# First batch of a two-layer transformer kernel: order of its first transfers, of the split of the values' weights, and of the weight ring's refill

## The reference, cut to what matters

```python
L0_attn: q, k, v = x @ wq.T, x @ wk.T, x @ wv.T        # 16 heads, 4 key/value heads, 128 wide
         q, k = rope(q), rope(k)
         o = chunked linear attention with decay per head; return o @ wo.T
L0_ffn:  W = (w_int - 128) * scale                     # gate, up: 2048 x 512, down: 512 x 2048
         return (silu(x @ Wg.T) * (x @ Wu.T)) @ Wd.T
L1_attn: 32 heads of 16, 8 key/value heads, causal softmax, rope on pairs
L1_ffn:  thought = layernorm(x)[:, -1] @ agg_w + agg_b; four steps of a small MLP on it
         out = layernorm(x + sigmoid(x @ gate_w + gate_b) * (thought @ bc_w + bc_b))
```

## Time and profile before

| | |
|---|---|
| median of three runs | 4269.03 us (4269.03, 4260.94, 4269.23) |
| profiled execution | 4257.74 us, span 4256.0 us |
| mean granted TensorE clock | 0.949 |
| data moved | 579.13 MB, mean 136 GB/s |

### The profile page before, as it was taken

The page is one execution under the profiler, slowest core; times in us unless marked ns, Lnnn a source line. Parts: engine busy times, 40 slices in busy tenths (PEclk is TensorE's granted clock), DMA queues, the critical chain, the costliest instruction groups (busy, mean ns, idle before and its releaser), DMA issues.

```text
span 4256.0 us, 53470 instructions
## 1 busy us (share of the span) xinstructions
PE 3761.6 (88%) x19048; PEld 2722.4 (64%) x19048; DVE 2366.8 (56%) x4206; ACT 1626.2 (38%) x2748; POOL 1352.6 (32%) x1637
## 2 busy tenths in 40 slices
PE   6877899999999999999999999999999999978640
PEld 4756676577766776577766776677757776654310
DVE  5644565455654665456654665456644665365369
ACT  4422334524353434434353434434353435423112
POOL 2421442235312441244212541145213531121125
PEclk9989999999999999999999999999999999987765
DMA  6456433254324433253324432343325441332313
GB/s 235 163 202 233 159 138 135 75 195 156 130 85 149 173 115 134 86 204 137 131 85 167 163 133 100 130 176 136 130 74 183 141 155 66 109 121 70 109 40 119
DMA packets 173764, 579.13 MB, mean 136 GB/s; under 512 B 14680, under 2 KB 14936, under 8 KB 168127
## 3 DMA queue, kind: packets, MB, share of 16 engines
q1 hardware_dynamic: 169806, 568.37, 37.4%
q10 hardware_dynamic: 3696, 7.34, 0.5%
HBM read 490.19 MB, written 84.93 MB: 135 GB/s over the span
## 4 chain that ended last, share of the span: by engine, by line
PE 67%; DVE 16%; ACT 6%; issue 5%; POOL 4%; DMA 2%; SPq 0%; DVEq 0%; ACTq 0%; POOLq 0%
PE ps_P L1720 25%; PE ps_Y L1720 11%; PE ps_E L1720 5%; PE ps_O L1720 4%; PE ps_O L1911 4%; PE ps_E L1893 3%; PE ps_T L1872 3%; POOL pT_lo L801 3%; PE ps_T L1720 3%; DVE pf L1278 2%; PE ps_T L1876 2%; ACT probs L1046 1%; DVE stats L1185 1%; ACT pT_hi L931 1%; DVE row_max L1386 1%
## 5 line engine op out<-in xcount | busy, mean ns | idle before, releaser
L1720 PE MATMUL ps_P<-XnT_hi,w_ring 128*128 128x512 f32 x3328 | 1080.2, 406 | 64.9 <-DVE XnT_lo L1161 14.5
L1720 PEld LDWEIGHTS ps_P<-XnT_hi,w_ring 128*128 128x128 f32 x3328 | 608.7, 191 | 230.1 <-issue 72.2
L1720 PE MATMUL ps_P<-XnT_lo,w_ring 128*128 128x512 f32 x1664 | 659.2, 396 | 0.0
L1386 DVE TENSOR_REDUCE row_max<-ps_T 128x1 fp32r<-128x384 f32 (+3 forms) x768 | 425.5, 595 | 275.9 <-PE ps_T L1876 275.8
L1046 ACT ACTIVATE probs<-ps_E 128x512 f32<-128x512 f32 (+2 forms) x768 | 362.5, 524 | 449.3 <-PE ps_E L1893 301.3
L801 POOL TENSOR_TENSOR pT_lo<-pf,pT_hi 128x512 fp32r<-128x512 f32 x320 | 411.2, 1293 | 300.3 <-ACT pT_hi L931 295.8
L819 POOL TENSOR_SCALAR_AFFINE_SELECT probs<-probs 128x512 f32<-128x512 f32 x256 | 163.2, 638 | 1031.8 <-ACT probs L1046 1031.8
L873 POOL TENSOR_TENSOR hT_lo<-hf,hT_hi 128x512 fp32r<-128x512 f32 x128 | 164.7, 1287 | 639.3 <-ACT hT_hi L931 639.3
L1720 PEld LDWEIGHTS ps_P<-XnT_lo,w_ring 128*128 128x128 f32 x1664 | 317.6, 191 | 70.8
L1720 PE MATMUL ps_Y<-w_big,hT_hi 128*128 128x512 f32 x896 | 333.3, 418 | 25.7 <-DVE y_acc L1410 12.6
L792 POOL TENSOR_TENSOR sines<-swapped,sinT 128x512 f32<-128x512 f32 x160 | 214.4, 1340 | 377.3 <-ACT swapped L931 369.0
(11 more groups left out here) (286 smaller groups left out, 7027.7 us busy)
## 6 DMA issues: line engine op xcount, KB each, us to landing
w_ring<-split_dram SPq DMA_DIRECT2D x412, 512.0 KB, 3.4
w_big<-split_dram SPq DMA_DIRECT2D x64, 2048.0 KB, 7.7
dec<-decay SPq DMA_DIRECT2D x32, 1024.0 KB, 4.9
split_dram<-w_ring SPq DMA_DIRECT2D x58, 512.0 KB, 4.1
split_dram<-w_big SPq DMA_DIRECT2D x36, 512.0 KB, 4.4
wo1w<-split_dram SPq DMA_DIRECT2D x8, 2048.0 KB, 7.7
gatew<-split_dram SPq DMA_DIRECT2D x7, 2048.0 KB, 9.8
X<-x SPq DMA_DIRECT2D x8, 1024.0 KB, 9.8
```

The lines of the kernel that those rows point to most:

```text
L1386: dve.reduce_max(row_max[:, g % 2, i_, m0:m0 + len(heads)], ps[TB[half]][:, 0:len(heads) * w].rearrange("p (n s) -> p n s", s=w), AX_X)\
L1720: last = pe.matmul(dst, stat[s_], mov[m_], start=first_ and k == 0, stop=last_ and k == n - 1)
```

## The change

- The first batch's tokens come as four transfers of 256 KB, each with a semaphore of its own; `ident` goes out behind the first of them on its own semaphore, and TensorE and ScalarE wait for that alone at the start.
- The rope tables are issued behind two raw pieces and ahead of the other two; the decay table behind "pro". The seven other constants are issued behind the last group's blocks, and waited for ahead of "ho" (ScalarE, VectorE) and in iteration 1 (TensorE).
- "pro" splits u0 to u7 only. V's four pieces are split behind units 0 to 3 of group 0, each after that unit's ring piece.
- In slots 36 to 43 of the first iteration SyncE waits until the slot's writes have landed and issues `next_unit` for that slot; the wait for all slots and the loop behind the 48 slots go.

```diff
 def first_pieces():
-    out = {("pro",): [("u", j) for j in range(RING)] + [("w", BIG_V, k) for k in range(4)]}
+    out = {("pro",): [("u", j) for j in range(RING)]}
...
-                out["p", g, u] = [("u", NU * g + u + RING)]
+                out["p", g, u] = [("u", NU * g + u + RING)] + ([("w", BIG_V, u)] if g == 0 and u < 4 else [])
...
-            tokens_in(0)
-            for dst, src in ((ident[:, :], identity), (mask[:, :], causal), (ident_b[:, :], identity_b),
-                             (rope1[:, :, :, :].rearrange("p a t d -> p (a t d)"), rope1_tables),
-                             (gate_bias[:, :], gate_b.partition_broadcast(P)), (dsc[:, :], down_scale.partition_broadcast(P)),
-                             (gsc[:, :], gate_scale), (usc[:, :], up_scale)):
-                sp.dma_start(dst, src).then_inc(const_in, 16)
-            for r in range(RAW):
+            for t in range(NT):
+                sp.dma_start(X[0][:, t, :], x[0, t * P:(t + 1) * P, :]).then_inc(*x0_in[t].hit(0))
+                if t == 0:
+                    sp.dma_start(ident[:, :], identity).then_inc(ident_in, 16)
+            for r in range(2):
                 piece_in(r)
             tables(0)
-            decay_in(0, 0)
+            for r in range(2, RAW):
+                piece_in(r)
             for n in range(NB + 1):
                 c = n - 1
                 if n == 0:
                     first(("pro",))
+                    decay_in(0, 0)
...
                     if n == 0:
+                        for dst, src in ((mask[:, :], causal), (ident_b[:, :], identity_b),
...
+                            sp.dma_start(dst, src).then_inc(const_in, 16)
                         first(("ho",))
...
                         if n == 0:
                             first(("slot", s))
+                            if q == NQ - 1 and i < 8:
+
+                                k = UNITS_A + UNITS_C + 8 * q + i
+                                slot = slot_of[0, k]
+                                sp.wait_ge(*unit_out[slot].need(unit_out[slot].dims[0] - 1))
+                                next_unit(n, k)
                             if s == SLOTS - 1:
-
-                                for slot in range(RING):
-                                    sp.wait_ge(*unit_out[slot].need(unit_out[slot].dims[0] - 1))
...
-                if n == 0:
-                    for k in range(UNITS_A + UNITS_C + 24, UNITS):
-                        next_unit(n, k)
...
-            act.wait_ge(const_in, N_CONST)
+            act.wait_ge(ident_in, 16)
...
                 if n == 0:
+                    act.wait_ge(const_in, N_CONST)
                     first(("ho",))
...
-            dve.wait_ge(const_in, N_CONST)
             for n in range(NB + 1):
                 c, d = n - 1, n - 2
                 if n == 0:
-                    dve.wait_ge(*x_in[0].need(0))
                     for t in range(NT):
+                        dve.wait_ge(*x0_in[t].need(0))
                         measure("xa", 0, t, X[0][:, t, :])
...
                 if n == 0:
+                    dve.wait_ge(const_in, N_CONST)
                     first(("ho",))
...
-            pe.wait_ge(const_in, N_CONST)
-            pe.wait_ge(act_const_in, 1)
+            pe.wait_ge(ident_in, 16)
...
+                if n == 1:
+                    pe.wait_ge(const_in, N_CONST)
+                    pe.wait_ge(act_const_in, 1)
```

More of the change, by code:

```diff
@@ L370, in raw, with tokens_at @@
             return (raw_a if r % RAW < 2 else raw_b)[:, r % 2, :]
-        const_in, act_const_in = sem("s_const_in"), sem("s_identr")
+        const_in, act_const_in, ident_in = sem("s_const_in"), sem("s_identr"), sem("s_ident_in")
+        x0_in = [count(f"x0_in{t}", 1, step=16) for t in range(NT)]
         pool_const = sem("s_pool_const")
         x_in = [count(f"x_in{n}", NB // 2, step=16) for n in range(2)]
+        def tokens_at(n):
+            return n // 2 - (n % 2 == 0)
         x2_out, x2_in = count("x2_out", NB, step=16), count("x2_in", NB, step=16)
@@ L515, in build @@
         block = ctx.enter_context(nc.Block())
-        N_CONST = 16 * 8
+        N_CONST = 16 * 7
         @block.sync
@@ L566, in tokens_in @@
             def tokens_in(n):
-                sp.dma_start(X[n % 2][:, :, :], x[n, :, :].rearrange("(t p) d -> p t d", p=P)).then_inc(*x_in[n % 2].hit(n // 2))
+                sp.dma_start(X[n % 2][:, :, :], x[n, :, :].rearrange("(t p) d -> p t d", p=P)).then_inc(*x_in[n % 2].hit(tokens_at(n)))
             def decay_in(n, g):
@@ L676, in _ @@
                     if n == 0:
+                        for dst, src in ((mask[:, :], causal), (ident_b[:, :], identity_b),
+                                         (rope1[:, :, :, :].rearrange("p a t d -> p (a t d)"), rope1_tables),
+                                         (gate_bias[:, :], gate_b.partition_broadcast(P)), (dsc[:, :], down_scale.partition_broadcast(P)),
+                                         (gsc[:, :], gate_scale), (usc[:, :], up_scale)):
+                            sp.dma_start(dst, src).then_inc(const_in, 16)
                         first(("ho",))
@@ L1430, in behind @@
                         if t == 0:
-                            dve.wait_ge(*x_in[(n + 1) % 2].need((n + 1) // 2))
+                            dve.wait_ge(*x_in[(n + 1) % 2].need(tokens_at(n + 1)))
                         measure("xa", n + 1, t, X[(n + 1) % 2][:, t, :])
```

## The result

The changed kernel takes 4255.03 us (median of 13 runs, 4247.53 to 4268.45), the kernel before in the same comparison 4267.78 (13 runs). The ratio is 0.9972, 95% interval 0.9962 to 0.9981: 12 us or 0.28% faster. The prediction was 4250, in a range that holds the measured time. 12 us gained stand against 16.0 forecast. One of the 13 runs before took 5294.37 us, a slow run, and the ratio is of fast runs alone.

The account below looks back on a forecast made before the run. The prediction took the kernel as bound by TensorE's matmuls, untouched by the change; 5.6 us at the start plus 10.4 from the ring made 16.0, from 4266 to 4250 us. The range was 4238 to 4262.

Parts of the forecast that it names:

- Ring: Passage to the second batch: slot-by-slot refill removes 7.85 us of waiting and keeps TensorE's clock up, 10.4 us gained.
- rival 3: Second batch's first projections: the waiting goes but the lower clock stays; 13.5 us gained in all, 4252.5; chance 0.12.
- Start: First batch up to its first blocks: values products end at 57.4 us instead of 63.04, 5.6 us gained.
- Front: First batch's token statistics: the fourth aggregate starts at 6.9 us instead of 11.69, 4.7 us gained.
- Constants late: Seven constants issued behind the last group's blocks land before their first reader, at no cost, with 18 us margin.
- Decay table among the pieces: First batch, behind "pro": the 1 MB table among the weight pieces delays V's last piece by 2.7 us.
- Pace of the pieces: First batch's weight loads and splits: a piece every 1.93 us, set by DMA; at 2.6 us the start gives nothing.
- rival 1: First batch's start: pieces slow to 2.6 us each, so the start gives nothing; 10.4 us in all, 4255.6; chance 0.24.
- Rival 4: First batch's start: ring unit, rope and raw buffer wait in a circle; kernel 9.6 us slower, 4275.6; chance 0.04.
- Values cold: First batch's four values products, after TensorE stands still: the first takes 4.60 us, all four 12.8 us.
- Rival 2: First batch's start: TensorE keeps its clock before the values, pieces take 1.7 us; 19.8 us gained, 4246; chance 0.12.
- Past the first blocks: From 63 to 404 us: engine order unchanged, so the start's lead passes through; later batches keep their length.

Follow-up runs that it names:

- e2: The changed kernel with the ring refill put back as before; 2.6 us (0.06%) under the kernel before, with an interval that includes no change.
- after again: The changed kernel, unchanged, run again for a second profile and more runs; median 4257.21 us.
- e1: The kernel before with the slot-by-slot ring refill alone; 9.8 us faster by the ratio, 11.4 by the medians.
- e5: The changed kernel with the first tokens as one 1 MB transfer, ident behind it; the fourth aggregate starts at 9.32 us.
- e3: The kernel before with tokens by tile and late constants only; ratio 0.9991 with an interval that reaches 1.0000.
- e10: The changed kernel with the decay table issued behind V's last piece; 4255.54 us in one timed run.
- e6: The changed kernel with the decay table issued ahead of "pro", as before the change; 4249.74 us.
- e9: Against the changed kernel: V split behind units 0 and 1, u5 to u9 behind units 2 to 4, later pieces behind later groups' units, decay first; 4248.15 us.
- e7: Against the changed kernel: "pro" splits five ring pieces, then V's four; u10 to u12 in group 0's blocks, decay first; first blocks at 55.15 us.
- e8: Against the changed kernel: "pro" splits five ring pieces, V's four behind units 0 and 1, u10 to u12 in group 0's blocks, decay first; first blocks at 52.58 us.
- e4: The changed kernel with V's four pieces back in "pro", decay table still behind "pro"; 3 to 5 us under the changed kernel by the medians.
- e6b: The same kernel as e6, timed again beside the changed kernel; 4254.81 us, against 4257.21 for the changed kernel.

## Why the prediction was right, and where it was wrong

**Ring, 10.4 us forecast: right.** D went from 30.16 to 19.86, 10.3 us, in every kernel with the new refill (19.69 to 19.86) and in none without it. The waiting went and the clock stayed up: rival 3, the lower clock that stays, is out. Nothing else became late; V's 2 MB, issued at 442.92, is not in the chain: the values products there wait for VectorE, as before.

**Start, 5.6 us forecast: wrong.** e2 gives 2.6 us, not clear of no change; by the marks it is 1.2 us (C is 63.5 in the mean of after, after again and e2, 64.7 in the mean of before and e1). Its terms:

- *Front, 4.7 forecast, 3.3 measured* (B 15.74 in the mean of the same three, 19.04 in that of before and e1). I took the four tiles to land as fast as one transfer of 1 MB. In the first profile their statistics start 1.1 to 2.1 us apart (3.65, 5.79, 6.89, 8.20), the fourth at 8.20, a little behind the bound of 7.9 that I had given. The DMA views of 0 to 6 us are in the last part. The Trainium skill, page "DMA: Bandwidth & Descriptors", section "Bandwidth", has 138 GB/s at 64 KB and 341 at 1 MB, from transfers issued by GpSimd, and no row between; the estimate from it, 1.3 us less for the front, is nearly what came (1.4). That the number fits may be chance, since SyncE issues the transfers here and other loads stand behind them. I had set it aside with a row in which 256 KB pieces moved at 389 GB/s, but there many transfers, 512 KB ones among them, were in flight. Where I would not follow the rule is in batching to 1 MiB: e5 did this and was later.
- *Constants late, 0: right.* With them late e3 has a C-B of 45.56, with them early the kernel before and e1 have 45.37 and 45.99, and the changed kernel's first piece of "ho" starts at 254.72, without a wait for the seven constants, the last of which is issued by 234.63.
- *Decay table among the pieces, 2.7 forecast, 5.2 measured* (C-B 47.8 against 42.5 with the table ahead). This is the largest error. I charged its bytes. It is in the one queue ahead of loads on which ScalarE and VectorE wait, and its place costs twice its bytes. e10 confirms that: the same bytes behind V3's piece cost the first blocks nothing.
- *Pace of the pieces, 1.93 us each: right where the table is out of the way.* e6's two pieces per unit take 3.79 us. With the table in the queue the eight pieces from u7 (27.11) to V3 (47.98) take 2.6 us each, the very pace at which rival 1 has the start give nothing, and 2.4 in the two other traces. The measured 4255.03 also lies nearest to rival 1's 4255.6. But its cause, rope's pace, is not what did it: e6 has the same rope work. Rival 4, a circle between rope and split, didn't come. In the changed kernel too the units on either side of the hole are 3.79 us apart (27.76 to 31.55 and 44.84 to 48.63).
- *Values cold, 12.8 forecast, 13.8 measured in the first profile* (5.49 + 2.90 + 2.72 + 2.73), 13.6 and 13.4 in after again and e2. The clock fell, as forecast, after TensorE had stood still from 41.4 to 49.86 (granted 0.50 from 46 to 50 us); the first product was longer than the 4.60 us that I took. In e9, after a wait of 4.14 us, the first product behind it took 4.60 and the next 2.73. Rival 2, a clock that is kept, is out.

The three misses are 1.4 + 2.5 + 0.8 = 4.7 us, against 5.6 - 1.2 = 4.4 us missing; what is left is under the ±1 us by which C differs between profiles of one kernel. The forecast's test, V3's split at 43 to 45, failed (49.8 in the changed kernel), and held in e6 (43.2), where the table is out of the way. Without the table in the queue, moving V's split is a gain: C-B 42.5 against 45.6 in e3.

**Past the first blocks.** The forecast let the lead pass through to the end of the batch, and named a change in the length of the later batches as a sign of being wrong. In the mean the lead does pass: from C to the last down product the traces with a changed start and unchanged blocks (all but e7, e8 and e9) take 374.4 us, before and e1 375.8. But single traces run from 372.0 to 377.9, and those two ends are the changed kernel's own two profiles. And that sign did come: from the second batch's first `v_hi` to the last batch's it is 2835.3 us before and 2841.7 and 2841.8 in the changed kernel, and the last batch behind it is longer too (last part). e2 and e4, each with a part of the change, have 2835.5 and 2835.3, the others from 2835.4 to 2840.2. The cause stays open.

**The time.** Of the 5.0 us between 4250 and 4255.03, 3.2 are the gain (16.0 forecast, 12.8 by the medians), and the shortfall is the start's. The other 1.8 are the base: 4266, chosen between the profiled time and the median, against 4267.8 measured. The range of 24 us held the result, but it would have held it with no gain at all from the start.

## What to carry to other kernels

A transfer that is moved can cost more than its bytes (here 5.2 us for 2.5 to 2.7 us of bytes) where it stands in a full queue ahead of small loads that an engine waits for; ask which loads are issued within the next few microseconds, and put the large one ahead of the stretch or behind its last needed load. Split and load first what the next consumer needs, in the order of need, and leave nothing extra in a stretch that is a chain between engines (here three extra pieces cost 3.7 us in the blocks, and 2.8 us more in the lower clock of the matmuls behind them). A wait at the end of a stage that guards several buffers at once is worth taking apart by buffer, and here it brought both the wait and the clock behind it.

## What the runs showed of the hardware

**The four 256 KB transfers moved more slowly than one of 1 MB.** DMA view, 0 to 6 us, in 40 slices of 0.15 us; GB/s in each. The kernel after:

```profile
GB/s 0 0 0 0 0 0 0 0 0 0 0 0 27 27 68 96 273 369 423 345 328 308 208 218 259 164 218 232 191 109 123 191 178 259 287 314 314 273 259 300
```

The kernel before, one transfer of 1 MB and the constants behind it, and then e5, one transfer of 1 MB and behind it the same loads as in the kernel after:

```profile
GB/s 2 0 0 0 0 0 0 0 0 0 0 0 41 27 82 177 109 109 177 218 396 410 382 369 410 369 410 396 410 423 410 369 423 396 389 304 313 321 352 372
```

```profile
GB/s 0 0 0 0 0 0 0 0 0 0 0 0 41 96 123 96 150 96 137 205 164 205 369 437 396 396 410 437 396 396 410 437 396 396 410 335 345 410 399 410
```

From 3.3 us on the 256 KB transfers, issued 0.47 us apart, and what is behind them move at 109 to 314 GB/s (27 to 396 in the second profile); the kernel before moves mostly 370 to 420 up to 5.2 us, and e5 335 to 437. The first tile of the four is nevertheless there 2.9 us after its issue.

**The clock scatters in stretches where TensorE is only partly busy.** The same code with the same data, 3755 to 3855 us in two windows (columns as in the table of windows above, the clock third from the end). The kernel before, then the kernel after:

```profile
3755.00:3805.00 50.00, 41.35 (x222) 33.25 (x222) 29.66 (x72) 10.43 (x18) 5.72 (x14) 0.90 0.24 78
3805.00:3855.00 50.00, 38.66 (x227) 20.11 (x227) 27.56 (x53) 21.70 (x45) 5.73 (x9) 0.79 0.26 85
```

```profile
3755.00:3805.00 50.00, 41.98 (x204) 33.58 (x205) 28.57 (x69) 9.26 (x16) 5.16 (x14) 0.81 0.24 73
3805.00:3855.00 50.00, 41.55 (x209) 22.24 (x207) 24.09 (x48) 18.11 (x37) 5.10 (x8) 0.64 0.26 85
```

The granted clock there was 0.90 and 0.79 in one execution and 0.81 and 0.64 in the other. The time from the last batch's first `v_hi` to the end was 950.9 us before and 962.3 after, but also 950.9 in e1 and 960.8 in e2, 954.4 in e6 and 962.5 in its repetition, which is the same kernel. e6 and e6b show that one kernel has both lengths. Over all fourteen traces the two kernels with the old start, before and e1, have 950.9, and the twelve with a changed start 954.4 to 962.5, so a share of the changed start in it is not excluded. Against it: those two profiled executions lie 7 to 10 us under their kernels' medians, so their usual runs are longer than these. What decides it stays open, and it is why a change of 3 us in the first batch can't be read from one profile's span, nor quite from eleven timed runs.
